# One cross-attention block with a gene-expression layer: the gene product in two 64-column halves, and a new order for every engine

## The reference, cut to what matters

```python
# x: (16, 128, 512)   ctx: (16, 128, 256)   positions: (16, 128, 2)
x = x + attention(layernorm(x), ctx, positions)      # 32 heads of 16, rotary positions
x = x + gene_layer(layernorm(x))

def gene_layer(x):
    xn = x * rsqrt(mean(x * x) + eps) * norm_w
    logits = xn @ Wc.T / max(temperature, 0.1)        # 1024 genes
    top_vals, top_idx = top_k(logits, 32)
    expr_w = softmax(top_vals)
    expressed = einsum('btk,btkc->btc', expr_w, genes[top_idx])   # 64 wide
    down = tanh(expressed @ Wd.T)
    up = expressed @ Wu.T
    return down * xn * up * scale
```

## Time and profile before

| | |
|---|---|
| median of 3 runs | 488.25 us (485.88 to 488.64) |
| profiled execution | 486.55 us, its span 484.8 us |
| PE busy | 430.7 us, 89% of the span |
| DVE busy | 391.1 us, 81% |
| ACT busy | 276.1 us, 57% |
| POOL busy | 254.2 us, 52% |

### The profile page before, as it was taken

The page is one execution under the profiler, slowest core; times in us unless marked ns, Lnnn a source line. Parts: engine busy times, 40 slices in busy tenths (PEclk is TensorE's granted clock), DMA queues, the critical chain, the costliest instruction groups (busy, mean ns, idle before and its releaser), DMA issues.

```text
span 484.8 us, 10898 instructions
## 1 busy us (share of the span) xinstructions
PE 430.7 (89%) x3866; PEld 339.6 (70%) x3866; DVE 391.1 (81%) x616; ACT 276.1 (57%) x420; POOL 254.2 (52%) x258
## 2 busy tenths in 40 slices
PE   0865689999999999999999999999999999997734
PEld 0753467778786877787777777777878777776523
DVE  3885537798898898989888989989898999886780
ACT  3875265757384675657475766584756655644211
POOL 0456347535755666565667585756658467041122
PEclk9987979999999999999999999999999999999876
DMA  8870624222334050414050322315051404000000
GB/s 256 274 197 3 111 60 84 57 47 54 66 68 77 24 121 26 97 45 97 35 98 31 81 60 54 88 30 112 23 119 34 88 24 88 24 23 1 22 22 22
DMA packets 82028, 34.48 MB, mean 71 GB/s; under 512 B 73152, under 2 KB 75216, under 8 KB 82000
## 3 DMA queue, kind: packets, MB, share of 16 engines
q1 hardware_dynamic: 80896, 32.79, 29.5%
q10 hardware_dynamic: 1104, 1.31, 0.9%
HBM read 12.86 MB, written 4.19 MB: 35 GB/s over the span
## 4 chain that ended last, share of the span: by engine, by line
PE 60%; DVE 12%; DMA 7%; issue 6%; ACT 4%; SPq 3%; DVEq 1%; POOLq 0%; POOL 0%; ACTq 0%
PE psum L1606 37%; PE psum L1751 4%; DMA x_ring<-x_dram 4%; PE psum L1697 3%; DVE top L1268 3%; PE psum L1823 3%; DVE stage_a L1277 3%; DMA qT<-parts 2%; DVE row_max L1206 2%; PE psum L1787 2%; PE psum L1728 2%; PE psum L1812 2%; SPq L338 2%; PE psum L1761 2%; PE psum L1841 1%
## 5 line engine op out<-in xcount | busy, mean ns | idle before, releaser
L1268 DVE MAX8 top<-stage_a 128x8 f32<-128x1024 f32 x64 | 78.4, 1225 | 10.6 <-ACT stage_a L787 9.1
L1206 DVE TENSOR_REDUCE row_max<-psum 128x8 f32<-128x1024 f32 x64 | 75.4, 1220 | 14.3 <-PE psum L1697 13.8
L464 POOL TENSOR_TENSOR qk_cos<-stage_b,cos_t 128x512 f32<-128x512 f32 x31 | 39.7, 1280 | 78.8 <-issue 39.4
L1277 DVE MATCH_REPLACE8 stage_a<-top,stage_a 128x1024 f32<-128x1024 f32 x64 | 77.4, 1209 | 0.0
L787 ACT ACTIVATE stage_a<-psum,rstd 128x512 f32<-128x512 f32 x32 | 22.0, 688 | 75.2 <-PE psum L1606 75.1
L751 ACT ACTIVATE stage_b<-psum 128x1024 f32<-128x1024 f32 x64 | 63.4, 1025 | 2.1 <-PE psum L1728 1.7
L510 POOL TENSOR_TENSOR stage_c<-stage_c 128x512 f32<-128x512 f32 x16 | 20.6, 1288 | 70.3 <-ACT stage_c L816 70.3
L1606 PE MATMUL psum<-wcT_h,yT_h 128*128 128x512 f32 x128 | 54.6, 427 | 2.9 <-DVE yT_l L1254 2.0
L1606 PE MATMUL psum<-wcT_l,yT_h 128*128 128x512 f32 x128 | 51.0, 398 | 0.0
L1606 PE MATMUL psum<-wcT_h,yT_l 128*128 128x512 f32 x128 | 50.9, 398 | 0.0
L485 POOL TENSOR_TENSOR parts<-turned,parts 128x512 f16<-128x512 f32 x31 | 36.8, 1187 | 24.8 <-issue 22.5
(11 more groups left out here) (135 smaller groups left out, 1054.1 us busy)
## 6 DMA issues: line engine op xcount, KB each, us to landing
out_dram<-x_ring SPq DMA_DIRECT2D x16, 256.0 KB, 2.0
x_ring<-x_dram SPq DMA_DIRECT2D x15, 256.0 KB, 2.6
ctx_sb<-ctx_dram SPq DMA_DIRECT2D x16, 128.0 KB, 2.4
stage_a<-L_ffn_Wc_dram SPq DMA_DIRECT2D x1, 2048.0 KB, 9.1
stage_b<-L_xattn_Wq_dram ACTq DMA_DIRECT2D x1, 1024.0 KB, 9.8
stage_b<-L_xattn_Wkv_dram SPq DMA_DIRECT2D x2, 512.0 KB, 7.8
stage_c<-L_xattn_Wout_dram SPq DMA_DIRECT2D x1, 1024.0 KB, 5.2
qT<-neg_maxT SPq DMA_DIRECT2D x32, 8.0 KB
```

The costliest lines, as they stand in the source:

```text
L464: pool.tensor_tensor(halves(qk_cos), halves(qk_sb), trig(cos_t, t), ALU.mult).then_inc(s_cosm[n], 1)
L1206: nc.vector.tensor_reduce(row_max[:, 0:HEADS].rearrange("p (odd m) -> p odd m", odd=2)[:, :, 4 * g:4 * g + 4], score_of[g][:].rearrange("p ...
L1268: nc.vector.max(top[:, 8 * n:8 * n + 8], logit if n == 0 else rest).then_inc(s_top[n], 1)
L1277: nc.vector.match_replace(rest, top[:, 8 * n:8 * n + 8], logit if n == 0 else rest, REMOVED).then_inc(s_rem[n], 1)
```

## The change

The gene product is made with a stationary operand of 64 columns: even blocks of genes write PSUM rows 0 to 63, odd blocks rows 64 to 127, each in its own half of the columns of the array. Both halves now hold partial sums, whose sum `down_up` takes by its duplicated weights; high and low parts need tiles of their own (`eT_h`, `eT_l`) and `down_up` takes three matmuls for each of down and up instead of two. The gene table is loaded once instead of twice; the room goes to a seventh slot of x. The load of the positions is the first DMA. The banks, the waits that guard them, and the order of all five engines are made anew. q is now projected one tile further ahead, and the logits, top-k and gene product stand about half a round later relative to the attention.

```diff
-XSLOTS = 6
+XSLOTS = 7
-        genes_sb = sb("genes_sb", [P, GK, 2 * GD])
+        genes_sb = sb("genes_sb", [P, GK, GD])
-        eT_hl = sb("eT_hl", [2 * GD, P], f32r)
+        eT_h, eT_l = sb("eT_h", [2 * GD, P], f32r), sb("eT_l", [2 * GD, P], f32r)
-        BANK = {"down": 2, "eT": 2, "gene_wT1": 2, "row_maxT": 2, "yT": 2, "ctxT": 3, "gene_wT0": 3,
+        BANK = {"k": 0, "q": 0, "logits1": 1, "xT": 1, "v": 2, "yT": 2, "eT": 3,
...
             def express(t):
...
-                for n in (1, 0):
+                for n in range(2):
                     pe.wait_ge(s_wTr[n], t + 1)
-                    for g in range(4 * n, 4 * n + 4):
-                        last = nc.tensor.matmul(bank("eT")[:, 0:P], genes_sb[:, g], gene_wT[:, g * P:(g + 1) * P],
-                                                start=(g == 4), stop=(g == 3))
+                for g in range(GK):
+                    rows = slice(GD * (g % 2), GD * (g % 2) + GD)
+                    last = nc.tensor.matmul(bank("eT")[rows, 0:P], genes_sb[:, g], gene_wT[:, g * P:(g + 1) * P],
+                                            start=(g < 2), stop=(g >= GK - 2))
...
-                nc.tensor.matmul(gene_out[n], eT_hl[:], wduT_h[:, cols], start=True, stop=False)
-                nc.tensor.matmul(gene_out[n], eT_hl[:], wduT_l[:, cols], start=False,
-                                 stop=True).then_inc((s_dn, s_upp)[n], 1)
+                nc.tensor.matmul(gene_out[n], eT_h[:], wduT_h[:, cols], start=True, stop=False)
+                nc.tensor.matmul(gene_out[n], eT_h[:], wduT_l[:, cols], start=False, stop=False)
+                nc.tensor.matmul(gene_out[n], eT_l[:], wduT_h[:, cols], start=False, stop=True).then_inc((s_dn, s_upp)[n], 1)
...
+            sp.dma_start(pos_raw[:], pos.rearrange("t p c -> t (p c)")).then_inc(s_pos, 16)
             load_ctx(0)
             sp.dma_start(wk_raw, wkv[:, 0:DIM].rearrange("(k p) n -> p k n", p=P)).then_inc(s_wk, 16)
-            sp.dma_start(pos_raw[:], pos.rearrange("t p c -> t (p c)")).then_inc(s_pos, 16)
```

More of the change, by code:

```diff
@@ new lines, in filling @@
+                transpose_attn(1)
+                project_v(3)
+                scoresT(2, 0)
+                scoresT(2, 1)
+                project_out(1)
+                scoresT(2, 2)
+                scoresT(2, 3)
+                values(2, 0)
+                values(2, 1)
+                transpose_ctx(4)
+                logits(0, 0)
+                logits(0, 1)
+                scores(3, 1)
+                scores(3, 2)
+                values(2, 2)
+                values(2, 3)
+                scores(3, 0)
@@ L1938, in filling @@
+                scoresT(3, 3)
+                scoresT(3, 2)
                 values(3, 0)
                 values(3, 1)
-                scoresT(3, 3)
-                scoresT(3, 2)
-                express(0)
-                transpose_x(5)
-                project_out(2)
-                down_up(0, 0)
-                project_q(5)
+                transpose_ctx(5)
+                project_v(4)
+                logits(1, 0)
+                logits(1, 1)
+                scores(4, 1)
+                scores(4, 2)
@@ L1960, in filling @@
-                logits(2, 1)
-                project_k(5)
+                express(0)
+                transpose_y(2)
+                transpose_attn(3)
+                down_up(0, 1)
+                down_up(0, 0)
+                project_q(6)
                 scoresT(4, 1)
                 scoresT(4, 0)
-                transpose_w(1, 1)
-                transpose_attn(3)
-                transpose_w(1, 0)
+                project_v(5)
+                scoresT(4, 3)
                 scoresT(4, 2)
@@ L1980, in filling @@
+                project_k(6)
+                scores(5, 3)
+                transpose_w(1, 1)
+                transpose_o(4)
+                transpose_x(7)
+                express(1)
+                transpose_max(5)
+                transpose_attn(4)
                 transpose_y(3)
+                project_q(7)
+                down_up(1, 0)
                 down_up(1, 1)
-                project_q(6)
-                scores(5, 0)
-                scores(5, 3)
-                logits(3, 0)
@@ L1999, in filling @@
-                scoresT(5, 3)
-                scoresT(5, 2)
             def iteration(i):
-                transpose_x(i - 1)
+                values(i - 3, 1)
+                transpose_ctx(i - 1)
                 project_out(i - 4)
-                down_up(i - 6, 1)
-                down_up(i - 6, 0)
-                project_v(i - 2)
-                project_q(i - 1)
+                logits(i - 5, 0)
+                logits(i - 5, 1)
                 scores(i - 2, 2)
-                transpose_y(i - 4)
+                scores(i - 2, 1)
@@ L2027, in iteration @@
+                scoresT(i - 2, 3)
                 values(i - 2, 0)
-                values(i - 2, 1)
-                scoresT(i - 2, 3)
-                scoresT(i - 2, 2)
-                express(i - 5)
             def draining():
-                transpose_x(15)
+                values(13, 1)
+                transpose_ctx(15)
                 project_out(12)
-                down_up(10, 0)
-                project_q(15)
+                logits(11, 1)
                 values(13, 2)
+                scores(14, 2)
@@ L2050, in draining @@
                 transpose_max(14)
+                express(10)
+                transpose_y(12)
+                transpose_attn(13)
+                down_up(10, 0)
+                down_up(10, 1)
+                scoresT(14, 0)
+                scoresT(14, 1)
+                values(14, 0)
+                values(14, 1)
+                scoresT(14, 3)
+                scoresT(14, 2)
+                project_out(13)
                 logits(12, 1)
-                project_k(15)
-                scoresT(14, 1)
+                logits(12, 0)
```

1232 lines of the change are left out of this document (609 added, 623 removed).

## The result

The changed kernel took **483.1 us** (median of 4 runs, 482.46 to 483.64), the kernel before, run beside it, 488.44 us (485.88 to 489.35). The ratio is 0.9908, with a 95% interval of 0.988 to 0.9936: about 1% faster, where 477 us had been forecast. The profiled execution took 482.9 us, its span 481.1 us (before: 486.55 and 484.8), so the sum of the prediction, -10.9 us, stands against -3.7 between the two profiled executions and -5.3 between the medians.

What follows compares the result with a forecast made beforehand. The prediction took PE's own work to bound the loop, DVE having time to spare. Loop -5.4, head -2 and tail -3.5 summed to -10.9 us from 486.55, 475.7 us profiled; the median was forecast at 477 us, range 468 to 487.

Steps and rivals of the forecast that it cites:

- The gene product: PE's product in each tile: half the columns, two beside each other, 0.95 us instead of 1.89, saving 0.94 us a tile.
- The rival that the halves don't run beside each other: Gene product on PE: stays at 1.9 us, so 488.5 us in all, no change; chance 0.05.
- `down_up`: Two more matmuls of 128x512 a tile on PE, 0.24 us each: +0.48 us.
- PE's own work: PE's work in a round: gene product, added matmuls and switches together, -0.18 us a tile.
- the term for switches: PE, each round: two more changes of the array's division and one more run of projections, +0.18 + 0.10 = +0.28 us.
- The order of the loop: Waits in the loop: PE's 0.37 us wait for `attn_lo` goes, 0.1 us of others comes, -0.27 us a round.
- The rival of one wait for another: Loop: the new order trades one wait for another of the same size; 483 us at the median; chance 0.12.
- k turned late: SP: k's turn behind the store comes too late for the scores; 495 us at the median, slower; chance 0.11.
- The filling part: Early tiles: under the loop's regime from about scores(3) on, counted within the loop's 12 rounds and -5.4 us.
- The head: Start until PE fills up: earlier transfers and first turn of q, -2 us, bounds +1.5 and -5.
- The tail: Drain after the last tiles: earlier residual, DVE's 2.77 us wait nearly gone, shorter last product; -3.5 us, bounds -0.5 and -5.
- last product, less the third `down` matmul: Tail: last gene product 1.8 us in halves instead of 3.64, less 0.4 for a third `down` matmul, -1.4 us.

Runs made afterwards that it cites:

- serial_halves: The changed kernel with the gene product's even blocks issued in a row, then the odd ones, instead of alternating; 490.14 us, ratio 1.0029.
- halves_only: The kernel before with the gene product in halves and three matmuls for each of down and up, old orders and banks; 489.13 us, ratio 1.0031.
- turns_together: The changed kernel with eight slots of x, and SP's store moved behind the two turns; 481.97 us, ratio 0.9853.
- xfirst_full: x_first with the gene product back at 128 columns and two matmuls for each of down and up; 483.73 us, ratio 0.9899.
- before_early_x: The kernel before, old orders and full-width product, with a seventh slot and the load of x ahead of both turns on SP; 486.36 us, ratio 0.9946.
- x_first: The changed kernel with the load of x ahead of both turns on SP and an eighth slot of x; 473.94 us, ratio 0.9721.
- halves_early_x: halves_only with a seventh slot and the load of x ahead of both turns on SP; 486.24 us, ratio 0.9965.

## Why the prediction was wrong

The direction was right. Of the forecast's 10.9 us, 3.7 came between the profiled executions, and of the 11.3 us that 477 promised, 5.3 between the medians. Two steps failed: that the loop is bound by PE's work and the load of x comes off the path, and that the drain gets 3.5 us shorter.

**The gene product** (-0.94 us a tile): right, 1.89 to 1.03 us. The rival that the halves don't run beside each other is refuted by serial_halves. The Trainium skill, "TensorE: Matmul & The Clock Gate", Part 3, says that a weight load overlaps matmuls in flight only when the row group differs; both halves use all the rows, so by that rule there is no gain from alternating, and the trace doesn't agree, with 1.03 us alternating against 1.51. The same page's section "Why this matters for your kernels" says that products of few columns, each on a column group of its own, gain as those on row groups do; with that the trace agrees.

**`down_up`** (+0.48): right; six starts 0.23 us apart.

**PE's own work** (-0.18 us): mis-sized, by the term for switches (+0.28). Between loops that are all PE's, the halves are worth 25.41 to 24.92, -0.49 us: the product's -0.92 and `down_up`'s +0.47 leave -0.04 for the product's own two changes of division, where +0.18 had been put down. The new order added nothing (25.47 to 25.41), where +0.10 had been put down for one more run of projections. Single prices can be read from rows, but added up over a round they gave a difference that isn't there.

**The order of the loop** (-0.27 us of waits): this step failed. It said that the load now opens the round and so comes off the path. In a loop the head of a round is the end of the one before: the load stands directly behind the two turns, and these had been moved behind `scoresT`. So the load is issued 6.8 us after the end of the last `scoresT`, and the new place of the mean, ahead of the maxima, carries the delay to PE. I had read the price of the chain from the one PE wait it left (0.37 us), and took "PE 99% busy" for "bound by PE's work". halves_only shows that it was not: 0.9 us less work outside the ring and 0.47 more inside gave +0.5 us a round. With the load moved, and only with it, the step comes out better than forecast: 25.79 to 24.92, -0.87 where -0.45 had been said. The bounds of the step, -0.9 and +0.1, don't follow from its terms either, which give -0.55 and -0.18; the measured +0.24 lies outside both.

**The rival of one wait for another** (0.12) said 483 us at the median, the number that was measured, and late maxima, which were seen. That the number fits is luck: the new wait is 1.07 us against 0.37 and not of the same size, the loop became longer, the filling part made up for it, and the drain gained nothing.

**k turned late**, the rival on the slower side, had the right queue and the wrong victim. The two turns on SP do hold something up, but it is the load of x behind them, not the scores; and the store's wait, its mechanism, is worth 0.2 us a round (turns_together).

**The filling part** gave more than was put down: from tile 3's to tile 7's scores 4.1 us, 3.0 between tiles 5 and 6 and 1.9 between tiles 3 and 4, with 0.9 lost again between the others. The other kernels bear it out (102.8 to 103.4 us in the old order, 97.9 to 99.3 in the new one with alternating halves), but no run took it apart.

**The head** (-2): the right way; that it reads -1.9 is in part luck, since the means over the kernels differ by 4 us. The positions' share can't be told.

**The tail** (-3.5): failed, +0.7. Its start had moved by 4.4 us, and tile 15's residual comes only 2.6 us earlier, at 442.17, than in the earlier trace rows, so the way to it became 1.8 us longer: the new order leaves the gene stage of one more tile in the drain. The wait of 2.77 us before the last tile's first scan is gone, as said, but it brought 0.8 us and not 2.8: from the residual to that scan it takes 13.0 us (442.17 to 455.16) where it was 13.7, since DVE now does 2 us more work in between: one more scan and one more removal of tile 14 are left. From the start of the last product to the end it takes 11.0 us where it was 11.8: the term "last product, less the third `down` matmul" (-1.4) gave 0.8, because of the clock. The three add up to the measured +0.7 (1.8 - 0.3 - 0.8), where -0.3 is the way from the residual to the last product.

The order and the halves can be told apart in two ways, and they don't add up alike. By xfirst_full and before_early_x the order costs the drain 5.2 us, and by xfirst_full and x_first the halves give 4.3 back. In the old orders the halves gave 3.1 us (halves_only, 73.6 from 76.7) or 1.6 (halves_early_x, 74.9 from 76.5), and with halves the new order costs 3.8 or 2.5. By either way the shortest drain is that of the old orders with the halves.

After the change, busy time and clock of the last transposes, product and `down_up`:

```profile
467.38:470.10 2.72, 1.96 (x8) 1.57 (x9) 0.14 (x1) 1.20 (x2) 0.00 (x0) 0.50 0.14 56
470.12:472.10 1.98, 1.98 (x16) 1.57 (x16) 0.00 (x0) 0.00 (x0) 0.00 (x0) 0.50 0.03 8
472.79:475.70 2.91, 2.91 (x6) 1.82 (x6) 0.00 (x0) 0.69 (x1) 0.46 (x1) 0.50 0.00 0
```

and before:

```profile
471.07:472.90 1.83, 1.82 (x8) 1.57 (x8) 0.15 (x1) 0.60 (x1) 0.00 (x0) 0.50 0.21 83
472.97:476.70 3.73, 3.70 (x17) 3.46 (x16) 0.00 (x0) 0.60 (x1) 0.00 (x0) 0.53 0.00 0
477.37:478.60 1.23, 1.19 (x4) 0.67 (x4) 0.00 (x0) 0.47 (x1) 0.00 (x0) 1.00 0.00 0
```

The product fell from 3.70 to 1.98 us, nearly all of it at 1.2 GHz before and all of it after. Before, the clock rose to 2.4 GHz at the end of the long product and `down_up` ran in 1.19 us; now it is still at 1.2 GHz and `down_up`, with six matmuls instead of four, takes 2.91. Together 4.9 us in both. Whether the shorter product is what kept the clock down isn't shown. It is down there in all kernels with halves, but also in xfirst_full, after a product of full width (product and `down_up`):

```profile
468.08:471.87 3.79, 3.75 (x16) 3.46 (x16) 0.00 (x0) 0.00 (x0) 0.00 (x0) 0.50 0.00 0
472.53:474.80 2.27, 2.08 (x4) 1.17 (x4) 0.00 (x0) 0.69 (x1) 0.24 (x1) 0.50 0.00 0
```

There, both at 1.2 GHz, the term can be checked: from the last product's start to the end it is 12.3 us in xfirst_full and 11.0 in the changed kernel, -1.3 where -1.4 had been put down. So the term was sound for one clock, and the clock was the mistake.

## What to carry to other kernels

Before pricing an edit in a software pipeline, find the ring of the round: follow the chain of waits through a whole round and ask of each edit whether it lies inside or outside. A small wait on an engine that is 99% busy may be all that shows of a ring as long as the round, and the next ring may lie right behind it. In a hand-written loop the first entry stands behind the last: a load with nothing to wait for belongs ahead of slow issues on its queue, not behind them. And an order that lets a stage lag by most of a round gets the bill in the drain.

## What the runs showed of the hardware

The issue of a transposing DMA holds SP for 2.07 us (q) and 2.53 us (k) in the round of the changed kernel shown above (medians of its 16 tiles 2.0 and 2.5), that of a plain load of 256 KB for 0.35 us; what stands behind two turns is 4.6 us late before anything is waited for.

An fp32 instruction of 64 columns (128 moving) is hardly cheaper by itself than one of 128: one starts every 0.109 us in serial_halves against 0.111 in xfirst_full. The gain comes from the other half working beside it: 1.03 us for the tile's eight blocks when neighbours alternate between the halves, 1.95 with 128 columns. Four blocks of one half and then four of the other still overlap in the middle and take 1.51.

The same short burst can end at either clock: `down_up` behind the last full-width product ran at 2.4 GHz in 1.19 us in the kernel before and in before_early_x, and at 1.2 GHz in 2.08 us in xfirst_full. A gain that is read at one clock holds at that clock only.
